# Attention and expert kernel on one core: a reordered prologue, and block 0's routing steps in smaller parts

## The reference

```
x = x + layernorm2(xl + attention(xl)) * gamma + beta      with xl = layernorm(x)
    attention: 16 heads of 64, q, k, v with biases, softmax(q k^T / 8) v, output projection
f = layernorm(x)
x = x + experts(f)
    s = sigmoid(f Wr^T); bias added; of 8 groups the best 4 (by their two best), then the best 8 of 64 experts
    coef = 2.5 * s / sum(s) over the chosen; sum over e of coef_e * (silu(f Wg_e) * (f Wu_e)) Wd_e, and a shared expert
```

## Time and profile before

| | |
|---|---|
| median of the runs | 1255.48 us |
| profiled execution | 1255.55 us, span 1253.8 us |
| mean granted clock of TensorE | 0.989 |
| busy: TensorE, VectorE, ScalarE, GpSimd | 97%, 85%, 71%, 79% |

### The profile page before, as it was taken

The page is one execution under the profiler, slowest core; times in us unless marked ns, Lnnn a source line. Parts: engine busy times, 40 slices in busy tenths (PEclk is TensorE's granted clock), DMA queues, the critical chain, the costliest instruction groups (busy, mean ns, idle before and its releaser), DMA issues. The chain is left out here.

```text
span 1253.8 us, 33479 instructions
## 1 busy us (share of the span) xinstructions
PE 1220.3 (97%) x12473; PEld 684.3 (55%) x12473; DVE 1066.4 (85%) x1965; ACT 885.6 (71%) x1586; POOL 991.7 (79%) x1218
## 2 busy tenths in 40 slices
PE   3999999999999999999999999999999999999998
PEld 0466666666666666666666644444444444444443
DVE  6788988888888998989999888787888878787875
ACT  4788877777777778787777666666667676667554
POOL 2788888888888999988888576868786877777665
PEclk7899999999999999999999999999999999999999
DMA  7455564665554655654565354444444444444442
GB/s 185 103 105 113 96 119 107 111 109 113 106 115 107 120 108 116 109 115 109 109 115 110 69 141 130 142 139 142 138 145 134 141 138 142 136 129 138 139 143 85
DMA packets 186862, 152.60 MB, mean 122 GB/s; under 512 B 104720, under 2 KB 143952, under 8 KB 186704
## 3 DMA queue, kind: packets, MB, share of 16 engines
q1 hardware_dynamic: 186704, 150.50, 51.1%
HBM read 80.16 MB, written 3.15 MB: 66 GB/s over the span
## 5 line engine op out<-in xcount | busy, mean ns | idle before, releaser
L1175 PE MATMUL bank<-arena 128*128 128x65 f16 (+2 forms) x12344 | 1209.9, 263 | 20.5 <-DVE arena L1055 7.1
L1175 PEld LDWEIGHTS bank<-arena 128*128 128x128 f16 (+1 forms) x12344 | 669.5, 98 | 548.5 <-issue 85.6
L570 POOL TENSOR_TENSOR arena<-arena 128x512 f16<-128x512 f32 x504 | 538.0, 1093 | 82.1 <-ACT arena L723 81.7
L608 POOL TENSOR_TENSOR arena<-arena 128x256 f16<-128x256 f32 x528 | 342.4, 675 | 132.3 <-ACT arena L784 125.7
L723 ACT ACTIVATE arena<-bank 128x512 f32<-128x512 f32 x512 | 291.8, 595 | 120.9 <-PE bank L1175 104.1
L1046 DVE TENSOR_REDUCE arena<-bank 128x2 f32<-128x1024 f32 x256 | 311.8, 1219 | 43.1 <-PE bank L1175 43.0
L1140 DVE TENSOR_TENSOR arena<-arena,bank 128x512 f32<-128x512 f32 x264 | 181.9, 689 | 61.9 <-ACT bank L779 38.9
L784 ACT ACTIVATE arena<-arena 128x512 f16<-128x512 f32 x264 | 164.7, 624 | 95.9 <-DVE arena L1140 94.0
L1132 DVE TENSOR_TENSOR arena<-arena,bank 128x512 f32<-128x512 f32 x256 | 173.9, 679 | 24.2 <-PE bank L1175 23.2
L779 ACT ACTIVATE bank<-bank 128x512 f32<-128x512 f32 x264 | 153.3, 581 | 55.3 <-PE bank L1175 55.1
L1055 DVE SCALAR_TENSOR_TENSOR arena<-bank,arena 128x512 f16<-128x512 f32 x128 | 95.5, 746 | 19.4 <-ACT arena L713 19.3
(11 more groups left out here) (106 smaller groups left out, 368.0 us busy)
## 6 DMA issues: line engine op xcount, KB each, us to landing
arena<-coef_rows SPq DMA_DIRECT2D x512, 128.0 KB, 2.9
arena<-arena SPq DMA_DIRECT2D x256, 128.0 KB, 2.5
arena<-arena SPq DMA_DIRECT2D x64, 256.0 KB, 3.1
arena<-in_L_attn_x SPq DMA_DIRECT2D x9, 256.0 KB, 3.5
arena<-in_L_ffn_Wg SPq DMA_DIRECT2D x32, 64.0 KB, 2.4
arena<-in_L_ffn_Wu SPq DMA_DIRECT2D x32, 64.0 KB, 2.2
arena<-in_L_ffn_Wd SPq DMA_DIRECT2D x32, 64.0 KB, 2.2
arena<-arena SPq DMA_TRANSPOSE x128, 3.4
```

Source lines behind the costliest of these rows:

```text
L570: last = pool.tensor_tensor(num_lo[:, u % 2, s, h, :], num[:, u % 2, s, h, :], num_hi[:, u % 2, s, h, :, 1], ALU.subtract)
L608: last = pool.tensor_tensor(hid_lo[:, r, at], hid[:, r, at], hid_hi[:, r, at], ALU.subtract)
L1175: return nc.tensor.matmul(out_, lhsT, rhs, start=start, stop=stop, skip_group_check=True)
```

## The change

In the prologue:

- Query and key weights are split in two parts: columns of pairs 0 and 1 of each batch first, the rest after the first block of x.
- Pair 0's five DMAs come in another order. Three of them count on a new semaphore, `first_rows`, and `maxima` of pair 0 waits for these three; the other two are waited for by ScalarE ahead of pair 2's query and by TensorE ahead of `scores(0)` of pair 0.
- Pair 1's products go to banks of their own (`ps_turn` and `ps8[2]`), and the waits for pair 0's low parts go. `maxima` of pair 0 uses two double banks in turn, as the others.
- In run -1 the negated row of pair 0 goes ahead of the key product of pair 2. In run 0 `scores(0)` goes ahead of the last maxima of pair 1.
- In run -2 VectorE's second low part goes from slot 2 to slot 1.
- The V and output weights are loaded in run -2, after pair 1's DMAs; ScalarE splits them at (-1, 3), VectorE at (0, 1).
- Statistics: 16 tiles at (-2, 1), 6 at (0, 0), 6 at (1, 0); the variance of all at (1, 2). The power on GpSimd is taken block by block, two runs ahead of each block's transposes, and the shift on VectorE one run ahead. The transposes stand in runs 4, 5, 6, 7, 9, 10 and 11.

In the routing: step 15 of block 0 is in three parts (add, and the reciprocal in two halves, the second at (51, EARLY)), step 23 in two halves, step 28 a slot later. Of block 1's routing, the steps from 4 to 14 come one tile later on every engine.

```diff
- (50, EARLY): ((15, 0),), (50, 1): ((15, 1),), (52, EARLY): ((16, 0),) ...
+ (50, EARLY): ((15, 0),), (50, 1): ((15, 1),), (51, EARLY): ((15, 2),), (52, EARLY): ((16, 0),) ...
- (58, 1): ((23, None),)
+ (58, EARLY): ((23, 0),), (58, 1): ((23, 1),)
- (62, 1): ((27, 1), (28, None))
+ (62, 1): ((27, 1),), (62, 2): ((28, None),)
-DVE_1 = {2: (1,), 3: (2,), 4: (3,), 9: (7,), 10: (8,), 14: (12,), 18: (16,), ...
+DVE_1 = {2: (1,), 3: (2,), 4: (3,), 10: (7,), 11: (8,), 15: (12,), 18: (16,), ...
-POOL_1 = {4: (3, 2), 6: (5,), 7: (6,), 10: (8,), 16: (14,)}
-ACT_1 = {5: (4,), 6: (5,), 11: (9, 10), 14: (11,), 16: (14,), 31: (30,)}
-PE_1 = {10: (8,), 12: (11,), 26: (27,)}
+POOL_1 = {4: (3, 2), 7: (5,), 8: (6,), 11: (8,), 17: (14,)}
+ACT_1 = {6: (4,), 7: (5,), 12: (9, 10), 15: (11,), 17: (14,), 31: (30,)}
+PE_1 = {11: (8,), 13: (11,), 26: (27,)}
...
         def max_bank(pair, q):
-            if isinstance(pair, int) and pair == 0:
-                return (bank[0], bank[2], bank[1], bank[0])[q]
             return (bank[0], bank[2])[q % 2]
         def proj_bank(t, which):
-            return ps8[1] if isinstance(t, int) and (t, which) == (0, 1) else ps_proj
+            return {(0, 1): ps8[1], (1, 0): ps_turn, (1, 1): ps8[2]}.get((t, which), ps_proj) if isinstance(t, int) else ps_proj
...
# SyncE
+                    if p == -3:
+                        a, b = flat[0:K, z, :, :], flat[K:P, z, :, :]
+                        sp.dma_start(stack[0:K, r, 0, Q1:Q2 + 1, :], a[:, ZQH:ZQH + 1, :].broadcast_to([K, 2, S])).then_inc(first_rows, 16)
+                        sp.dma_start(stack[0:K, r, 0, K1:K2 + 1, :], a[:, ZKH:ZKL + 1, :]).then_inc(first_rows, 16)
+                        sp.dma_start(stack[K:P, r, 1, Q1:K1 + 1:2, :], b[:, ZQH:ZKH + 1, :]).then_inc(first_rows, 16)
+                        sp.dma_start(stack[K:P, r, 0, Q1:K1 + 1:2, :], a[:, ZQL:ZKH + 1:2, :]).then_inc(stacked[odd], 16)
+                        sp.dma_start(stack[0:K, r, 1, :, :], b).then_inc(stacked[odd], 16)
-                if p == -3:
+                if p == -2:
                     load_vo()
-                if p == -2:
                     load_rest()
...
# GpSimd
-            deviations(slice(QT, NT), A_VAR1)
+                    if s == 1 and isinstance(p, int) and (p + 2, 0) in TURN_AT:
+                        n = TURN_AT[p + 2, 0]
+                        deviations(slice(n * QT, (n + 1) * QT), A_VAR1)
...
# ScalarE
-            step(nc.scalar.activation(wq_hi, raw_q.rearrange("p (n c) -> p n c", n=HP), ACT.Copy, scale=K ** -0.5))
-            step(nc.scalar.activation(wk_hi, raw_k.rearrange("p (n c) -> p n c", n=HP), ACT.Copy))
+            weights_qk_hi(0, 2)
             hi_block(0)
+            weights_qk_hi(2, HP)
...
-                if (p, s) == (-1, 1):
+                if (p, s) == (-1, 3):
                     act.wait_ge(in_vo, 2 * 16)
...
                         act.wait_ge(max_scores, 4 * (t - 2) + 1)
+                        if isinstance(t, int) and t == 2:
+                            act.wait_ge(stacked[0], 2 * 16)
...
# VectorE
-            weights_lo(wq_lo, wq_hi, raw_q, K ** -0.5)
+            weights_lo(wq_lo, wq_hi, raw_q, K ** -0.5, 0, 2)
+            dve.wait_ge(act_step, ACT_QK)
+            weights_lo(wk_lo, wk_hi, raw_k, 1.0, 0, 2)
             lo_block(0)
-            weights_lo(wk_lo, wk_hi, raw_k)
+            weights_lo(wq_lo, wq_hi, raw_q, K ** -0.5, 2, HP)
+            weights_lo(wk_lo, wk_hi, raw_k, 1.0, 2, HP)
...
-                if (p, s) == (-2, 1):
+                if (p, s) == (1, 2):
                     variance(QT, NT, A_VAR1)
-                if (p, s) == (-1, 2):
+                if (p, s) == (0, 1):
                     weights_lo(wv_lo, wv_hi, raw_v)
-                if (p, s) == (-1, 3):
                     weights_lo(wo_lo, wo_hi, raw_o)
...
-                if (p, s) == (0, 3):
-                    dve.wait_ge(a_rstd, 2)
...
+                if s == 0 and (p + 1, 0) in TURN_AT:
+                    dve.wait_ge(a_rstd, n + 1)
...
+                        half = scores(m)[:, (part - 1) * QT // 2:part * QT // 2, :]
+                        last = nc.vector.reciprocal(half, half)
...
# TensorE
                     if q0 == 0:
-                        pe.wait_ge(stacked[up % 2], 80 * (half + 1))
+                        if pair == 0:
+                            pe.wait_ge(first_rows, 3 * 16)
+                        else:
+                            pe.wait_ge(stacked[pair % 2], 80 * (pair // 2 + 1) - (0 if pair % 2 else 3 * 16))
...
-                        if not valid(p, -1):
-                            wait(pe, qk_lo, 2 * t)
+                        if t == 2:
+                            pe.wait_ge(qk_lo, 1)
+                            pe.wait_ge(dve_step, W_READY)
+                        elif t > 2 and not valid(p, -1):
+                            pe.wait_ge(qk_lo, 2 * t)
...
                     if s == 0:
+                        if p == 0:
+                            pe.wait_ge(stacked[0], 2 * 16)
+                            scores(0)
                         maxima(p + 1, u + 1, 2)
-                        scores(0)
+                        if p != 0:
+                            scores(0)
...
+                        if p == -1:
+                            negated_row()
                         project(1)
...
-STATS_AT = {(-3, 2): (QT, 14), (-3, 3): (14, 20), (-2, 0): (20, 26), (-2, 1): (26, NT)}
-TURN_AT = {(n + n // 2 + 1, 0): n for n in range(1, B)}
+STATS_AT = {(-2, 1): (QT, 20), (0, 0): (20, 26), (1, 0): (26, NT)}
+TURN_AT = {(4, 0): 1, (5, 0): 2, (6, 0): 3, (7, 0): 4, (9, 0): 5, (10, 0): 6, (11, 0): 7}
```

More of the change, by code:

```diff
@@ L429, in run @@
                     sp.wait_ge(qk_lo, 2 * t + 2)
-                    for h in range(2):
+                    if p == -3:
[5 more added lines that the diff above has]
+                        sp.dma_start(stack[0:K, r, 1, :, :], b).then_inc(stacked[odd], 16)
+                    for h in range(2 if p > -3 else 0):
                         a = flat[h * K:(h + 1) * K, z, :, :]
@@ L742, in run @@
                         exponential(3)
+                        if isinstance(p, int) and p == -1:
+                            copy_row()
                         if valid(t):
@@ L745, in run @@
                     if s == 2:
[L746 to L750, removed]
+                        if not isinstance(p, int) or p != -1:
+                            copy_row()
                         exponential(4)
@@ L959, in route @@
                 if k == 15:
-                    if first_half:
+                    if part == 0:
                         dve.wait_ge(logit_exp, 1)
                         nc.vector.tensor_scalar(scores(m), scores(m), 1.0, None, ALU.add).then_inc(logit_sum, 1)
-                    if second_half:
+                    else:
+                        half = scores(m)[:, (part - 1) * QT // 2:part * QT // 2, :]
                         dve.wait_ge(logit_sum, 1)
-                        nc.vector.reciprocal(scores(m), scores(m)).then_inc(sigm, 1)
+                        last = nc.vector.reciprocal(half, half)
+                        if part == 2:
+                            last.then_inc(sigm, 1)
                 g8 = sfc(m).rearrange("p t (g e) -> p (t g) e", g=G)
@@ L1093, in run @@
                         normalise(0)
+                        if isinstance(p, int) and p == -2:
+                            low(1)
                     if s == 2:
                         row_max(p + 2, u + 2, 0)
-                        low(1)
+                        if not isinstance(p, int) or p != -2:
+                            low(1)
                         row_max(p + 2, u + 2, 1)
@@ L1349, in context, with negated_row @@
                         last.then_inc(ctx_ps, 1)
+                def negated_row():
+                    if not valid(p, 1):
+                        return
+                    if p == -1:
+                        pe.wait_ge(qk_lo, 3)
+                    wait(pe, y_added, p - 4 + 1)
+                    pe.wait_ge(negmax_done, p + 1 + 1)
+                    if (p, 0) in TURN_AT:
+                        pe.wait_ge(tr_a_lo, TURN_AT[p, 0] + 1)
+                    if p == LOGITS_AT - 1:
+                        pe.wait_ge(tr_c_lo, 1)
+                    if p == LOGITS_AT:
+                        pe.wait_ge(logit_exp, 1)
+                    for k in range(QT):
+                        last = mm(ps_turn[:, k * P:(k + 1) * P], negmax[:, k, :], ident16, True, True)
+                    last.then_inc(maxrow_ps, 1)
                 for s in slots:
                     if s == 0:
+                        if p == 0:
+                            pe.wait_ge(stacked[0], 2 * 16)
+                            scores(0)
                         maxima(p + 1, u + 1, 2)
-                        scores(0)
+                        if p != 0:
+                            scores(0)
                         project(0)
@@ L1364, in run @@
```

(2 more changed lines are left out.)

84 lines of the change are left out of this document (46 added, 38 removed).

## The result

The changed kernel takes 1260.17 us (median of 5 runs, 1259.43 to 1261.41) against 1255.48 before (1254.57 to 1255.93 in these 5 runs): ratio 1.0038, 95% interval 1.0027 to 1.005. It is slower by 4.7 us. The forecast of 1253.7 and its range (1251.0 to 1256.5) both miss. The profiled execution took 1259.70, span 1257.7: 4.15 and 3.9 more than the one before.

The account below looks back on a forecast made before the run. TensorE, busy 97% of the span, was taken as the bound. From 1255.55 us, prologue -3.0, clock +1.7, new work +0.4 and block 0's routing -0.9 gave -1.8, so 1253.7 us, range 1251.0 to 1256.5.

Parts of the forecast that it names:

- prologue, shift of scores(5) of pair 0: Prologue: the score matmul waiting for pair 2's half maximum starts at 40.85 instead of 43.84, -3.0 us.
- clock at the restart: TensorE restarting at scores(5) of pair 0: half rate after a hole costs +1.7 us (0 to 2.8).
- new work of pairs 0 to 9: Moved statistics and variance on VectorE in pair 1 make a half maximum late: +0.4 us (0 to 1.0).
- routing of block 0: Pair 50 on: halved reciprocal and mask multiplication, later last product, shrink TensorE's wait: -0.9 us (-0.4 to -1.2).
- tables of block 1: Block 1's routing shifted by one tile: costed at 0 us (-0.5 to +0.4).
- a variance of seven small operations: VectorE in pair 1: the seven were priced at 1.2 us together, as in the earlier prologue.
- nothing waits for pair 2's rows: Prologue transfer queue: loads ahead last till about 29.6, and the rows are asked for at 30.2, so no wait.
- (a): Rival: clock holds through the hole ahead of scores(5), or the hole is smaller; 1252.0 us, chance 0.31.
- rival (c): Clock stays at 1.2 GHz through pairs 0 and 1, making the kernel slower; middle 1258 us, chance 0.09.
- A hole in pair 1 over 0.5: Sign that the forecast is wrong: TensorE holes over 0.5 us in pair 1.

Follow-up runs that it names:

- e1: Changed kernel, with GpSimd waiting ahead of its third subtraction of pair 1 until VectorE's variance is done: 1256.28 us.
- e2: Changed kernel without the seven variance operations of pair 1, constants standing in for mean and variance of blocks 1 to 7: 1253.99 us.
- e7: Changed kernel, with four aggregates and one addition per block, two runs ahead of its transposes, instead of the seven variance operations: 1259.01 us.
- e6: e3 plus seven unread matmuls ahead of scores(5) of pair 0, and the router's transposes moved from slot 1 to slot 2: 1253.28 us.
- e10: e9 with shared weights loaded as in the changed kernel, six statistics moved to pair 0's last slot, plus e6's seven matmuls and later transposes: 1250.42 us.
- e3: Changed kernel, with the last 12 statistics and the variance moved to run -1, where GpSimd is idle: 1254.81 us.
- e9: Changed kernel, variance of blocks 1 to 4 in run -1, blocks 5 to 7 by aggregates in run 2, Wo remainder and shared/first expert loads moved: 1254.27 us.

## Why the prediction was wrong

| step | predicted | measured in the changed kernel |
|---|---|---|
| prologue, shift of scores(5) of pair 0 | -3.0 | -3.1 (43.84 to 40.74) |
| clock at the restart | +1.7 | +1.8 (half of 40.74 to 44.30) |
| new work of pairs 0 to 9 | +0.4 | +5.45 (pair 1 to pairs 6 and on) |
| routing of block 0 | -0.9 | -0.7 (pair 44 to pair 63) |
| tables of block 1 | 0 | +0.1 |
| sum | -1.8 | +3.9 span, +4.15 profiled time |

The measured terms add to 3.55. Of the rest of the span, 0.20 came in between scores(5) of pair 0 and pair 1 (-1.3 to -1.12) and 0.20 at pair 44 (+4.33 to +4.53); neither was explained.

**The step that failed** is "a variance of seven small operations (1.2, as from 22.03 to 23.22)", and with it "+0.4 (0 if TensorE still runs at half rate there, 1.0 if the variance adds in full)". The duration was taken from a place where GpSimd was idle and used in a place where it is not. The seven took 5.2 there (e1 shows why), the lateness became a hole of 3.92 and not of 0.56, and the hole cost another 1.46 by the clock, a term that the prediction had for the prologue alone. The bound of 1.0 "in full" was no bound: the operations were five times their price.

The trace of before held a row that warned of it, in the pairs where block 0 is routed (timeline, VectorE and GpSimd):

```profile
697.59 4.09 POOL L570 TENSOR_TENSOR arena<-arena 128x512 f16<-128x512 f32 x4
699.87 0.83 DVE L1030 TENSOR_SCALAR arena<-arena 128x4 f32<-128x4 f32 x1
```

Four columns in 0.83 us, where the same operation on 28 took 0.18 at 23.04. L1030 runs eight times in the kernel, and the other seven have no GpSimd instruction beside them (min/median/max in ns):

```profile
L1030 DVE TENSOR_SCALAR arena<-arena x8: 170/170/830, 699.9 to 1171.3; 128x4 f32<-128x4 f32 x8
```

Beside L1030's first execution GpSimd's third subtraction ends at 697.59 + 3 x 1.02 = 700.66, the operation at 700.70: most of that is no work but a wait, and as a price it would have given 7 x 0.83 = 5.8. The Trainium skill (SBUF — State Buffer, Who interferes with whom) states the rule: VectorE and GpSimd share a pair of ports as an exclusive lock; a VectorE operation with two inputs in SBUF contends with a GpSimd operation that reads SBUF, and for whole instructions. L859 to L861 agree (up to 1.07 beside GpSimd, 0.20 without). That section of the Trainium skill lets tensor_scalar contend only in a two-port mode; which mode ran is in no trace, but L862 and L867 took 0.94 and 0.95 here and 0.18 in e1.

**The prologue** came out right, partly by errors that cancel, and partly by luck in which execution was profiled. Four traces have this prologue unchanged: the changed kernel, e1, e2 and e7. Scores(5) stands at 40.74, 39.86, 41.07 and 41.55 there, 2.3 to 4.0 earlier than before and 3.0 in the mean; the low clock behind it costs 1.8, 0, 2.6 and 2.8. So the two terms of the prediction are right as means, and their sum is anything from -4.0 to +0.5. In the changed kernel's trace, the maxima of pair 0 began at 19.27 instead of 20.5 and those of pair 1 at 27.27 instead of 28.25. That microsecond was lost again: the two weight remainders took 3.48 beside GpSimd's subtractions, not the 2.44 of the earlier trace rows (the same wrong price a second time), and ended at 39.5 as predicted. Between operations as long as these GpSimd pays too: two of its seven subtractions took 2.02 there. The sentence that nothing waits for pair 2's rows was wrong: the issue for gamma alone took 3.00, the queue was behind until past 31, and TensorE waited 2.11. I read this as a cost to the clock and not to the point, since the half maximum at 39.47 stands behind the remainders.

**The clock** did in this execution what the prediction says: up within the dense stretch (34.06), down in a hole of 2.11, 0.50 at the restart, back 3.6 us later. The hole was another one, though: pair 2's rows ended it, for which "nothing waits", and not VectorE. In e6 and e10, without such a hole, the clock holds; in e1 it holds through holes of 1.34 and 0.94, and holes of 2.5 go either way (e2, e3).

**Routing**: the reciprocal's half took 0.95 (0.9 predicted) and the hole closed.

**The rivals.** In e1's execution the clock was 1.00 at the restart, as (a) has it. The time of the changed kernel fell where rival (c) had put it (1258 to 1260), but not by its mechanism: it needed a low clock until 48 at least, and the clock was up at 44.30. A hole in pair 1 over 0.5 was named as what would make the prediction wrong; it is what did, for a reason that no rival had.

## What to carry to other kernels

Price a small VectorE operation by what GpSimd does at the place it is moved to, not by its duration at the place it comes from: look for the same form beside a busy GpSimd, and where a few columns take as long as a GpSimd instruction, each such operation costs one of them. Small chains belong where GpSimd is idle, and a chain that stands ahead of something TensorE needs can be paid twice: here 3.92 of hole and 1.46 of low clock. When the start of a kernel is rearranged, follow GpSimd's and SyncE's order past the edit as carefully as TensorE's: e9 lost most of pair 0's gain where GpSimd waited for one load that came later.

## What the runs showed that was not expected

- Beside a stream of GpSimd subtractions, VectorE gets about one small SBUF operation through per subtraction: five of the seven took 0.78 to 1.07 us instead of the 0.18 to 0.20 that they take alone; the subtractions stay at 1.034 to 1.041.
- Aggregates of statistics (four in 0.37 us) run beside the same subtractions without a wait.
- With seven matmuls whose result nobody reads, and the router's transposes moved, the kernel was faster and its runs more alike: 1253.28 with a spread of 1.1 us against 1254.81 with 3.2. Which of the two did it was not taken apart.
- A hole of about 2.5 us let the granted clock fall in one execution (e2) and not in another (e3).
